# Drains of TensorE carry the increments of hand-offs, and POOL's sends wait for TensorE no more

## What is computed

```python
x = x + layernorm(attn(layernorm(x), W_act, W_val, W_rec))   # scan over time, then W_val and a gate
x = x + layernorm(ffn(layernorm(x), gate_w, w1, w2, shared_gate_up, shared_down))

def ffn(x):                                        # 1024 tokens, 64 experts, 6 of them for each token
    probs = softmax(x @ gate_w.T)
    topk_w, topk_idx = top_k(probs, 6)
    h = silu(einsum('th,eih->tei', x, experts_w1)) # inner width 176
    y = einsum('tei,ehi->teh', h, experts_w2)
    g, u = split(x @ shared_gate_up.T, 2)
    return combine(y, topk_idx, topk_w) + (silu(g) * u) @ shared_down.T
```

## Time and profile before

| what | value |
|---|---|
| runs without a profile, median of 3 | 280.43 us (279.81 to 282.03) |
| span of the profiled execution | 287.2 us |
| TensorE busy in it | 236.9 us (82%) |
| VectorE busy | 175.1 us (61%) |
| POOL busy | 128.2 us (45%) |

### The profile page before, as it was taken

The page is one execution under the profiler, slowest core; times in us unless marked ns, Lnnn a source line. Parts: engine busy times, 40 slices in busy tenths (PEclk is TensorE's granted clock), DMA queues, the critical chain, the costliest instruction groups (busy, mean ns, idle before and its releaser), DMA issues.

```text
span 287.2 us, 4231 instructions
## 1 busy us (share of the span) xinstructions
PE 236.9 (82%) x1382; PEld 178.1 (62%) x1382; DVE 175.1 (61%) x552; ACT 81.5 (28%) x188; POOL 128.2 (45%) x162
## 2 busy tenths in 40 slices
PE   6978939976398884349878898999999989989990
PEld 6534818552153663227666687888888858758880
DVE  4539896989997857261308698753433333443884
ACT  2586631384021145000012222112222411120033
POOL 7008300004776574654767326566565654561000
PEclk9999998999599999576979999999999997999998
DMA  6999999997322232445298999999959732668913
GB/s 225 349 376 371 371 369 421 421 417 308 106 106 84 88 115 83 162 146 164 102 290 291 394 314 344 339 377 340 361 180 350 256 119 75 219 222 271 348 42 110
DMA packets 34615, 72.00 MB, mean 251 GB/s; under 512 B 4576, under 2 KB 24608, under 8 KB 34080
## 3 DMA queue, kind: packets, MB, share of 16 engines
q1 hardware_dynamic: 29024, 55.68, 55.8%
q0 software_dynamic: 5568, 16.03, 14.9%
HBM read 44.89 MB, written 26.80 MB: 250 GB/s over the span
## 4 chain that ended last, share of the span: by engine, by line
PE 49%; DVE 19%; issue 13%; DMA 6%; another core or an unknown queue 4%; SPq 3%; ACT 3%; POOL 2%; ACTq 0%; POOLq 0%; DVEq 0%
PE bank L959 9%; PE bank L933 7%; PE bank L955 5%; PE bank L772 4%; PE bank L943 4%; PE bank L1023 4%; PE bank L976 4%; PE bank L790 4%; DMA early<-x_slots 3%; PE bank L781 3%; DMA x_slots<-rows,slot_i 3%; PE bank L842 2%; DVE stats L1088 2%; SPq L392 2%
## 5 line engine op out<-in xcount | busy, mean ns | idle before, releaser
L615 POOL DMA_INDIRECT y_rows<-zbuf,token_i x66 | 64.2, 973 | 50.8 <-DVE zbuf L1425 35.6
L567 POOL DMA_INDIRECT x_slots<-rows,slot_i x48 | 47.0, 980 | 61.9 <-DVE slot_i L1240 34.9
L1425 DVE COPY zbuf<-bank 128x256 f32<-128x256 f32 x66 | 24.7, 419 | 59.0 <-PE bank L959 45.3
L721 ACT ACTIVATE sgu_sb<-bank 128x256 f32<-128x256 f32 x33 | 12.6, 383 | 111.8 <-remote 56.2
L933 PE MATMUL bank<-work,w_all 128*128 128x128 f32 x256 | 35.9, 292 | 2.9 <-issue 2.1
L933 PEld LDWEIGHTS bank<-work,w_all 128*128 128x128 f32 x256 | 33.5, 207 | 3.7 <-issue 3.6
L959 PE MATMUL bank<-w_all,sgu_sb 128*128 128x256 f32 x128 | 35.3, 412 | 0.0
L976 PE MATMUL bank<-ident,early 128*128 128x128 f32 x128 | 21.1, 294 | 14.7 <-DMA early<-x_slots 12.8
L1409 DVE COPY work<-bank 128x512 f32<-128x512 f32 x33 | 22.5, 684 | 12.9 <-PE bank L976 9.9
L808 PE MATMUL bank<-x2nT,sgu_sb 128*128 128x256 f32 (+3 forms) x72 | 23.9, 481 | 7.4 <-DVE nt L1358 7.4
L959 PEld LDWEIGHTS bank<-w_all,sgu_sb 128*128 128x128 f32 x128 | 23.5, 197 | 10.0 <-issue 7.6
(11 more groups left out here) (218 smaller groups left out, 353.7 us busy)
## 6 DMA issues: line engine op xcount, KB each, us to landing
w_all<-pairs SPq DMA_DIRECT2D x32, 752.0 KB, 8.4
x_slots<-hidT SPq DMA_DIRECT2D x8, 1152.0 KB, 12.4
early<-x_slots SPq DMA_DIRECT2D x64, 144.0 KB
w_all<-y_rows SPq DMA_DIRECT2D x4, 1024.0 KB, 6.4
w_all<-y_rows SPq DMA_DIRECT2D x4, 512.0 KB, 10.4
y_rows<-zbuf,token_i POOLq DMA_INDIRECT x66
x_sb<-x SPq DMA_DIRECT2D x4, 256.0 KB, 3.6
out<-work SPq DMA_DIRECT2D x4, 256.0 KB, 2.1
```

The lines of the kernel that those rows point to most:

```text
L567: return pool.indirect_dma_start(x_slots, bass.IndirectOffsetOnAxis(ap=slot_i[:, c, k:k + 1], axis=0), rows[:, c, :], None)
L615: pool.indirect_dma_start(y_rows, bass.IndirectOffsetOnAxis(ap=token_i[:, s % 32:s % 32 + 1].bitcast(U32), axis=0), yS[:, s % 8, :], None) ...
L1425: dve.tensor_copy(yS[:, s % 8, :], y_b[s % 4][:, 0:C]).then_inc(y_done, 1)
```

## The change

TensorE gets a function `arrived`, which issues a drain and puts the increment on it. It takes the place of the increment on the last matmul in `turn_unit`, `logits` and `rank` for groups 1 and 2, in `product_v` for its last two pairs, in `gate_up` from its fourth part on, in `counts`, and in `turn_rows`, `rest` and `output` for the units outside of `QUADS`. In `turn_unit` one drain adds 2 behind both halves where each half added 1. POOL's nine waits for TensorE go; those for `slot_done` and for earlier sends stay.

```diff
             for n, (k, c) in enumerate(FIRST):
-                if n == 14:
-                    pool.wait_ge(v_ps, 4)
-                elif n == 19:
-                    pool.wait_ge(x2T_ps, 4)
-                elif n == 21:
-                    pool.wait_ge(rank_ps, 2)
                 if n >= 3:
                     pool.wait_ge(sent_first[n % 3], 16 * (n // 3))
...
             for n, (k, c) in enumerate(SECOND):
                 if n == 6:
-                    pool.wait_ge(rank_ps, 3)
                     pool.wait_ge(slot_done, 3)
-                elif n == 13:
-                    pool.wait_ge(tx_ps, 1)
-                elif n == 16:
-                    pool.wait_ge(h_ps, 1)
-                elif n == 18:
-                    pool.wait_ge(tx_ps, 2)
-                elif n == 22:
-                    pool.wait_ge(y_ps, 1)
-                    pool.wait_ge(tx_ps, 3)
-                elif n == 24:
-                    pool.wait_ge(y_ps, 2)
-                    pool.wait_ge(tx_ps, 4)
...
+            def arrived(signal, n=1):
+
+                pe.drain().then_inc(signal, n)
+
...
-                    mm.then_inc(x2T_ps, 1)
+                    if u == 0:
+                        mm.then_inc(x2T_ps, 1)
+                if u > 0:
+                    arrived(x2T_ps, KC)
...
-                mm.then_inc(v_ps, 1)
+                if k < 2:
+                    mm.then_inc(v_ps, 1)
+                else:
+                    arrived(v_ps)
...
-                mm.then_inc(lg_ps, 1)
+                if u == 0:
+                    mm.then_inc(lg_ps, 1)
+                else:
+                    arrived(lg_ps)
...
-                if g == 1:
+                if g == 1 and n < 3:
                     mm.then_inc(gu_ps, 1)
+                elif g == 1:
+                    arrived(gu_ps)
...
+                if u == 0:
+                    mm.then_inc(rank_ps, 1)
+                else:
+                    arrived(rank_ps)
...
-                mm.then_inc(count_ps, 1)
+                    pe.matmul(count_b[:, 0:E], ones[:], mask[:, t, :], start=(t == 0), stop=(t == NT - 1))
+                arrived(count_ps)
...
+            def alone(t):
+
+                return not QUADS[0] <= t < QUADS[1]
+
...
-                mm.then_inc(h_ps, 1)
+                if alone(t):
+                    arrived(h_ps)
+                else:
+                    mm.then_inc(h_ps, 1)
...
-                    mm.then_inc(y_ps, 1)
+                    if alone(t):
+                        arrived(y_ps)
+                    else:
+                        mm.then_inc(y_ps, 1)
...
-                mm.then_inc(tx_ps, 1)
+                if alone(t):
+                    arrived(tx_ps)
+                else:
+                    mm.then_inc(tx_ps, 1)
```

More of the change, by code:

```diff
@@ L822, in rank @@
                               start=False, stop=False)
-                pe.matmul(rank_b[:, E * a:E * z], ones[:], expert8[:, 0:z - a, :].rearrange("p c e -> p (c e)"),
-                          start=False, stop=True).then_inc(rank_ps, 1)
+                mm = pe.matmul(rank_b[:, E * a:E * z], ones[:], expert8[:, 0:z - a, :].rearrange("p c e -> p (c e)"),
+                               start=False, stop=True)
+                if u == 0:
+                    mm.then_inc(rank_ps, 1)
+                else:
+                    arrived(rank_ps)
             def counts():
@@ L830, in counts @@
                 for t in range(NT):
-                    mm = pe.matmul(count_b[:, 0:E], ones[:], mask[:, t, :], start=(t == 0), stop=(t == NT - 1))
-                mm.then_inc(count_ps, 1)
+                    pe.matmul(count_b[:, 0:E], ones[:], mask[:, t, :], start=(t == 0), stop=(t == NT - 1))
+                arrived(count_ps)
             def keep_warm(b, n):
```

## The result

The changed kernel is slower: its median is 292.07 us (288.21 to 296.12) against 281.02 us. The forecast was 278.0 us, its range 271.5 to 286.5. The profiled execution of the changed kernel took 288.21 us; its span is 286.5.

A forecast was written before the change was run, and what follows sets the result against it. The prediction took TensorE as the bound from 164 us on. Gains of 4.5 us (pauses) and 7.7 us (signals) less 9.8 us for drains made 2.4 us off 280.43: 278.0 us, range 271.5 to 286.5.

The forecast's parts named there:

- What bounds the kernel: From 164 us on TensorE is full, so a microsecond it loses there is a microsecond of the end.
- The pauses: POOL's waits for TensorE among its sends: taking them out was to bring 0.83 + 2.12 + 1.6 = 4.5 us.
- the 0.83 us for unit 1's rows: POOL's second send list, wait at send 13: the part lying ahead of send 15, which unit 1's rows need.
- first list: POOL's waits in its first send list: removal gains nothing directly, as POOL must stop for `slot_done` 2 behind them anyway.
- The late signals: Matmul signals reach consumers late while POOL issues indirect DMAs; increments on drains were to win 0.9 + 1.7 + 1.5 + 3.6 = 7.7 us.
- the second rival: Late signals belong mostly to the profile, so the 7.7 us can't be won: 285.7 us, chance 0.17.
- The price of a drain: A full TensorE stop: 0.26 us behind most pieces, 0.17 us behind `rest`; 39 drains that cost, 9.8 us.
- By place: Drain costs by stretch: tail 4.6 us, units 0 to 5 4.2 us, ahead of `rank(1)` and `rank(2)` 1.0 us.
- The head's 0.7 us for half clock: Units 0 to 5: five drains fall into the half-clock stretch from 127.8 to 134.6, costing half more, 0.7 us.
- The cheap stop: Rival, chance 0.20: signals on time and drains at 0.10 us each, 8.3 us less, 272.1 us.
- The late drain: Rival, chance 0.18: the drain's increment is as late as the matmul's, about 9 us slower, 289.7 us.
- Delays of the profile: Rival, chance 0.17: late signals come mostly with profiling; 4.5 us gained against 9.8 us of drains, 5.3 us slower.

The follow-up runs named there:

- the second execution: The kernel before, unchanged, run and profiled once more: 280.08 us, ratio 0.998; the span of its profiled execution is 279.7 us.
- the run with the waits ahead: Kernel before without POOL's pauses, with drains only in the tail and the next piece's semaphore waits ahead of them: 282.19 us, ratio 1.0045.

## Why the prediction was wrong

**What bounds the kernel** held. A microsecond that TensorE loses in the tail is one of the end: 7.1 us in the stretch and 0.8 us at either side of it, 8.7 us, are the surplus of the run with tail drains (7.3 to 8.7).

**The pauses**, forecast at 4.5 us, are worth 4.2 us by the ratio of one run and 5.6 us by that of the other (0.015 and 0.020 of 280.6). The mechanism is the one named: a wait for rows of about 2 us, and half clock behind it, which lasted 6.5 us and not the 3.5 us of the earlier trace rows. So the size came out from terms that differ: 2.26 + 3.25 us in the second execution for 2.12 + 1.6, and the 0.83 us for unit 1's rows is not seen apart. That the first list gains nothing, and that the later sends gain only through rows, held too.

**The late signals** are the first step that failed. The 7.7 us were counted from the earlier trace rows, and those rows are true of that execution only. The working said that its 287.2 us stood 6.8 us above the median, put that down as an offset to be taken off, and then took a gain out of the same 6.8 us. The offset was larger still: in every other profiled execution the span is 1.7 to 1.8 us shorter than the time of the same run, so a span of 287.2 us stands for some 289 us, where the other timed runs of this kernel lie between 278.5 and 283.0 us. In the second execution increments on matmuls come within 0.05 us, and there is nothing to win. The link to POOL's DMAs was read too widely as well. POOL was not issuing in all four places: at the last `product_v` it idled from 85.57 to 87.69 and at `rank(2)` for the 3.14 us ahead of 110.49, while their consumers started at 87.44 and 108.83:

```profile
84.61 0.96 POOL L567 DMA_INDIRECT x_slots<-rows,slot_i  x1 [0.30 <-DMA x_slots<-rows,slot_i]
87.69 0.95 POOL L567 DMA_INDIRECT x_slots<-rows,slot_i  x1 [2.12 <-PE bank L790]
```

That the signals were not late outside one execution was the second rival, held at 0.17; the argument against it, that one profile can't tell, spoke for neither side.

**The price of a drain** is the second. 0.26 and 0.17 us were taken, with 0.36 as the upper end; in the tail it is 0.40. The lost overlap was right (0.16 us behind turned rows, 0.07 us behind `rest`). The restart of 0.10 us, read at 58.92 in the earlier trace rows, was mis-sized: there TensorE's queue already stood at the wait for the copy. Behind a drain in the loop the gap is 0.23 to 0.25 us, because waits that used to be passed early now come after it (0.14 us of it, by the run with the waits ahead). The prediction's own list said "gaps of 0.2 to 0.3 us", which with the lost overlap would already have been 0.36 to 0.46.

By place: the tail was put at 4.6 us and is 7.3 to 8.7; the head at 4.2, and is 2.2 to 3.6; ahead of the loop 1.0, and is 1.4 to 2.4 by the traces. The head's 0.7 us for half clock was misread: of its drains only that behind unit 1's rows, which was counted as free, and that behind `rest(1)` fall into 127.8 to 134.6, not five. So it is the tail, where nothing hides a stop, that carries the miss. Part of it is the last drain, which was costed at nothing since only scatters stand behind it. But TensorE itself goes on to the shared expert: in the trace a register load, register operations and a branch of its sequencer run from 254.13 to 255.41 behind that drain, and in the kernel before, second execution, they were done while matmuls ran (245.31 to 246.90, with the last `output` ending at 247.92).

With both steps mended the sum comes out: no gain from signals, 4.5 us from the pauses as forecast, and 13.5 us for the drains by the run with the pauses put back (0.048 of 280.5) make 9.0 us more than before, a ratio of 1.032 where 1.031 was measured. The three places alone make 1.025; where the other 0.006, less than the noise, was lost is not shown.

**The rules named.** "PSUM — Partial Sum Buffer", section "Engine vs sequencer instructions", of the Trainium skill says to attach the increment to the producing matmul, as a matter of correctness; for time this case agrees, 0.982 with it and 1.031 with drains. The Trainium skill, "TensorE: Matmul & The Clock Gate", section "Single matmul latency", has roughly 175 ns as the fixed part of the array's draining, to which it adds the streaming of the columns; by that figure the drains would have cost an estimated 6.8 us. The measurement, 13 to 14 us, decides, and by the run with the waits ahead a third of a stop in the tail is semaphore waits.

**The rivals.** The cheap stop fell with the 0.40 us. The late drain fell with the increments above: behind a drain the silu of the single units starts 0.07 us after `rest`, behind a matmul 0.05. Delays of the profile came true, though of one profiled execution and not of profiling, and the rival's 285.7 us was still short by the drains' price.

**What the profile was to show.** Sends at 0.30 us but for the two named above, the last one 4 to 8 us earlier (6.69, and 4.97 against the 138.19 of the second execution of the kernel before), prompt silu, no wait of 2.12 us at unit 5's rows, no half clock at 144.8: these are there. Gaps of 0.2 to 0.3 us: behind most drains of the loop, but not behind every drain; ten of those ahead of it have 0.08. Units of 4.2 us in the tail: no, 4.81.

## What to carry to other kernels

Before counting a gain from waits in one trace, lay that execution's own time beside the runs: when it is several us longer, the waits may be the difference, and a second trace can settle it. A drain in a full TensorE stream costs the overlap of two pieces and every wait and register operation that the sequencer would have passed early; here 0.40 us each in the tail, so it belongs only where TensorE waits anyway; if it must stand elsewhere, the next piece's waits go ahead of it (0.14 us less each). Take the two halves of a change apart: here leaving out the pauses alone gives 0.98, and the drains undo it more than twice over.

## What the runs showed of the hardware that was not expected

- A second drain right behind the first costs 0.08 us; the stop that a drain makes in the tail costs 0.40 us: over the three drains of a unit 0.13 us on average is lost overlap (0.16, 0.16 and 0.07), and 0.24 us the gap behind it, of which 0.14 are semaphore waits; the rest lies in the pieces, which take a little longer behind a stop (`main` 1.13 instead of 1.06 us).
- Where most drains have no wait of their own behind them, a stop is cheaper: from the turning of group 1's tokens to the end of `counts` twelve drains made 19.4 us of 17.1, 0.2 us each.
- Whether short stops keep the clock low stays open. With stops of 0.23 us at the pieces of the head TensorE stayed at 1.2 GHz until 135.6 us in one trace, where it rose at 128.9 and 132.2 us in two traces without them whose `main(0)` starts at the same time; but it rose at 130.1 and 139.9 us in two traces of the changed kernel.
- One of the 14 profiled executions, the first of the kernel before, had increments of matmuls late by up to 6.5 us from the head to the tail, its paired units included, and was 7.5 us longer than the second of the same kernel. Nothing in the runs shows what set it off.
